# A single-core adaLN block with a top-2 expert layer: column halves asked for first in a tile, a shift leaves its bank at once, VectorE's work at the swiglu's begin spread out, slots' factors made ahead

## The chip, the cores and the metric

The kernel runs on one core of one Trainium2 chip. The metric is the device time of one launch in microseconds (us), the median of three runs. TensorE (PE) multiplies, VectorE (DVE) and ScalarE (ACT) work on rows of 128 partitions, GpSimd (POOL) and SyncE (SP) mostly issue DMAs.

## What is computed

The reference, cut to what matters (x has 4096 rows of D = 512, in two sequences; mod has six rows of 512 for each sequence):

```
sa, ca, ga, sb, cb, gb = rows of silu(c) @ wmod
ga, gb: |.| at least 0.25, sign kept
h = layernorm(x) * (1 + ca) + sa
# attention part, on h
qkv = rms(h) @ w_qkv.T ; q, k, v ; q, k = rms(q), rms(k)
w = exp(k)
y = sigmoid(q) * cumsum(w * v) / (cumsum(w) + 1e-6)
u, g = split(y @ w_swiglu.T)
x = x + ga * (h + u * silu(g) @ w_out.T)
# expert part
h = layernorm(x) * (1 + cb) + sb
gates = softmax of the 2 largest of 8 logits (h @ gate_w)
routed = sum over the 2 experts of gate * (gelu(h @ w1[e] + b1[e]) @ w2[e] + b2[e])
shared = gelu(h @ shared_w1 + shared_b1) @ shared_w2 + shared_b2
x = x + gb * (routed + shared)
```

All is fp32. Each product is made of three matmuls of rounded parts: both operands are split into a high part (ACT) and a low part (DVE), and PE multiplies hi*hi, lo*hi and hi*lo.

## The kernel before

Each engine has its own list of instructions, written out by hand in one order; engines wait for each other through semaphores. An instruction that waits holds back all that stands behind it on its engine. Memory is laid out by hand, too. The program has these stages, in order of time.

**Attention**, to about 365 us: 32 groups `g` of 128 rows. PE makes the products of a group, turns w and e by transposes (L761, `sums`), and ACT and DVE make norms, exponentials and cumulative sums. The six mod rows are made at the begin (`mod_row`, L716). For each sequence q a gain row and a shift row, spread over 128 partitions, stand in PSUM banks until DVE (`gain_a`, L1422) and ACT (`take_shift`, L1108 to L1110) copy them. The first call of `sums` on PE puts its transposes into those banks, so it waits for both copies of sequence 1. ACT calls `take_shift(1)` in its loop over groups at g == 1, behind `columns_hi(2)`.

**Swiglu**, to about 1456 us: passes "b" and "c" over the two halves of the swiglu's width, each with 8 tiles `t` of 512 rows and 8 blocks `s` of the width. For each block PE does 24 up products (L697 to L699), DVE multiplies the two halves (`s_t`, L1622), ACT rounds (`s_hi`), DVE makes `s_lo` (L1625), PE does 12 down products (L702 to L704) for the block before. In pass b, DVE has side work in fixed blocks of a tile: `rows_for_b(q)` at a sequence's first tile (the gain of the residual, `fix_gain` L1648 to L1651, then two products, L1659 and L1660), `token_stats` (L1631 to L1644) at s == 2, and `first_residual` at s == 3 to 6, whose last product is needed at the end of a tile. New weights come in pieces in the first tile (`w_blk`, L1418).

**Shared MLP**, about 1456 to 1676 us: 8 tiles of 512 rows, 4 blocks of the width each. The columns of the second norm's output are read back from HBM (`xs <- columns`, 1 MB) in halves of a tile, `load_half(h)` on SP (L518 to L527), h = 2t and 2t + 1, into three buffers. A load waits until PE has used up the half that the buffer held (`xs_free`), and in SP's list it stands behind other loads and stores: the rows `graw`, `h_rows`, the residual out and in (`second_norm_out`, `r_t`), `columns` (`hT_out`). The last tile's second norm (`LAST`) is finished here: PE turns rows to columns (`rows_to_hT`, L869), which waits for DVE's low part of the piece before (`hT_lo`, L1874), since both use one bank; in DVE's list `hT_lo(LAST, 2)` and `hT_lo(LAST, 3)` stand in tile 1 behind `block_s(1, 0)` and `block_s(1, 1)` (`s_lo`, L1922), and these behind `evacuate_s(0)` (L1684, L1688), which waits for the residual rows `r_t`. POOL meanwhile makes the lists of slots.

**Routed experts**, about 1676 us to the end: 71 slots of 128 rows for one expert. Each slot is gathered (POOL), turned on PE (L938), multiplied up (L951, L953), turned (L965), multiplied down (L979 to L981), and scattered with an add (POOL). On DVE `slot_o(j)` first makes the row `gb_row` (L2012: the gain row of the slot's sequences) in one buffer, waiting for the product before (`o_ok`), then waits for the down product, then multiplies into `o_t` (L2024).

Of the kernel before, what the change touches and what calls it, by code (L numbers as in the profile page):

```python
# [12 lines left out]
ALU = mybir.AluOpType  # L13
# [3 lines left out]
P = 128  # L17
# [18 lines left out]
def build(nc, x_tok, c, wmod, w_qkv, w_swi, w_sh, w_exp, b1s, b1r, b2p, b2s, gate_w, ident, tri, rank, tokid, ebase,  # L36
          thr, jota, steps, dues, jcol_in, list0, zrows, out):
    N, D = x_tok.shape
# [5 lines left out]
    NSUB = TT // P  # L44
# [41 lines left out]
    with ctx:  # L86
# [74 lines left out]
        NR = len(rows_t)  # L161
        o_t = [at(f"o_t{i}", k, [P, D]) for i, k in enumerate((180, 164, 166, 168, 170, 182, 128, 130, 132, 134))]
        NO = len(o_t)
        gb_row = at("gb_row", 174, [P, D])
        gT_hi = at("gT_hi", 184, [P, 2, H], F32R)
        gT_lo = at("gT_lo", 186, [P, 2, H], F32R)
        p_t = [at(f"p_t{i}", 188 + 2 * i, [P, D]) for i in range(2)]
        late_rows = [o_t[0], o_t[5], p_t[0], p_t[1]]
        u_t = at("u_t", 200, [P, 2, H])
        gl_t = at("gl_t", 202, [P, 2, H])  # L170
# [192 lines left out]
        def _(sp):  # L363
# [192 lines left out]
            sp.wait_ge(ffn["c"].ev_ok, NSUB * NT)  # L556
            sp.dma_start(b2_raw[:, :], b2p).then_inc(b_in, 16)
            gates_in(0)
            second_norm_out(LAST)
            for t in range(NT):  # L560
                if t == 1:
                    hT_out(LAST)
                if t == 4:
                    gates_out(LAST)
                    sp.dma_start(due_t[:, :, :], dues.rearrange("p (k j) -> p k j", k=3)).then_inc(tb_in, 16)
                if t == 3:
                    gates_out(LAST - 1)

                    sp.wait_ge(b2_ok, 1)
                    load_gain(1)  # L570
                if t + 1 < NT:
                    gates_in(t + 1)
                if t < LAST:
                    if t > 0:
                        load_half(2 * t + 2)
                    load_half(2 * t + 3)
                else:
                    half_left(2 * LAST - 2)
                    sp.dma_start(b1r_t[:, :], b1r).then_inc(b_in, 16)
                sp.wait_ge(ffn["s"].ev_ok, NSUB * (t + 1))  # L580
                sp.dma_start(tokens(out, t), r_t[:, :, :]).then_inc(out_st, 16)
                sp.wait_ge(out_st, 16 * (t + 1))
                if t < LAST:
                    load_r(x1_dram, t + 1)
# [468 lines left out]
        def _(act):  # L1053
# [143 lines left out]
            for g in range(NG):  # L1197
                square(g, 0)
                if g + 1 < NG:
                    columns_hi(g + 1)  # L1200
                if g == 0:
                    for n in range(1, NSUB):
                        square_h(n)
                    seed_root(0)
                if g == 1:
                    take_shift(1)
                if g in A_TURNS:
                    piece_hi(B0 + A_TURNS.index(g))

                t, n = g // NSUB + 1, g % NSUB  # L1210
                if g == 2:
                    square_h(NSUB)
                if 2 <= g < NG - NSUB + 1:
                    square_h(g + NSUB - 1)
                if g > 0 and n == 0:
                    seed_root(g // NSUB)
                    if t < NT:
                        seed_spread(t)
                square(g, 1)
                seed(g)  # L1220
                exponential(g, 0, w_t)
                exponential(g, 1, e_t)
                if g == 0:
                    seed_spread(1)
                if g >= 1:
                    reciprocal(g - 1)
                if g + 2 * NSUB < NG:
                    spread_of(g + 2 * NSUB)
                if 1 <= g < 5:
                    take_row(g + 1)  # L1230
                if g == NG - 2:
                    split(x_in, 16)
# [140 lines left out]
        def _(dve):  # L1373
# [279 lines left out]

            def rows_for_b(q):
                dve.wait_ge(bc_in, 16 * (4 if q == 0 else 6))
                if q == 0:
                    fix_gain(ga_t[0], tmp[0])
                    fix_gain(ga_t[1], tmp[1])
                then(nc.vector.tensor_tensor(a1_t[:, :], a1_t[:, :], ga_t[q][:, :], ALU.mult))  # L1659
                then(nc.vector.tensor_tensor(b1_t[:, :], b1_t[:, :], ga_t[q][:, :], ALU.mult))  # L1660

# [215 lines left out]
            for p in "bc":  # L1877
                for t in range(NT):
                    for s in range(NB):
                        if p == "c" and t >= 1 and s >= 5:  # L1880
                            hT_lo(t - 1, s - 5)
                        block_bc(p, t, s)
                        if p == "b":
                            if t == 0 and s == 0:
                                denominator(NG - 1)
                                sum_kv(NG - 1)
                            if t == 0 and s == 2:
                                quotient(NG - 1)
                                rows_for_b(0)
                            if t == T_SEQ and s == 2:  # L1890
                                rows_for_b(1)
                            if s == 2:
                                dve.wait_ge(r_in, 16 * (t + 1))
                                token_stats()
                            if 3 <= s < 3 + NSUB:
                                first_residual(t, s - 3)
                            if t == 0 and s == 7:
                                nc.vector.memset(prev[:, :, :], 0.0)
                                gate_weights()
                        else:  # L1900
                            hooks_c(t, s)
                        for i in pieces_at(p, t, s):
                            piece_lo(i)
                    if p == "c" and t >= 1:
                        hT_lo(t - 1, 3)
                    if (p, t) != ("c", LAST):
                        split(NC * (NT * PASS[p] + t + 1))
                    evacuate(p, t)
# [95 lines left out]
            def expert(j):  # L2004

                return dve.value_load(tab[0:1, 1, j:j + 1], min_val=0, max_val=(E - 1) * H)

            def slot_o(j):

                if j >= 1:  # L2010
                    dve.wait_ge(rt.o_ok, j)
                nc.vector.scalar_tensor_tensor(out=gb_row[:, :], in0=gbd_t[:, :], scalar=late_t[:, j:j + 1],  # L2012
                                               in1=gbs_t[0][:, :], op0=ALU.mult, op1=ALU.add).then_inc(rt.gr_ok, 1)
                dve.wait_ge(rt.gr_ok, j + 1)
                dve.wait_ge(rt.dn, j + 1)
                if j == 1:
# [5 lines left out]
                if j >= NO:  # L2022
                    dve.wait_ge(sc_st[(j - NO) % NA], 16 * ((j - NO) // NA + 2))
                nc.vector.scalar_tensor_tensor(out=o_t[j % NO][:, :], in0=bank_o[j % 2][:, :], scalar=gate_t[:, j:j + 1],  # L2024
                                               in1=gb_row[:, :], op0=ALU.mult, op1=ALU.mult).then_inc(rt.o_ok, 1)


            dve.wait_ge(b_in, 32)
# [14 lines left out]
            for j in range(NSLOT):  # L2043
# [8 lines left out]
                    slot_g(j + 1)  # L2052
                if j in R_TURNS:
                    piece_lo(R0 + 14 + R_TURNS.index(j))
            slot_o(NSLOT - 1)


# [70 lines left out]
```

## Time and profile before

| what | value |
|---|---|
| median of 3 runs | 1939.67 us (1938.92 to 1943.29) |
| profiled execution: device time | 1936.98 us |
| profiled execution: span of the core | 1935.2 us, mean granted TensorE clock 0.995 |
| PE busy | 1893.0 us (98%) |
| DVE busy | 1279.0 us (66%) |
| ACT busy | 650.1 us (34%) |
| POOL busy | 284.7 us (15%) |

The profile is one execution; its span is the time from its first to its last instruction, its device time has 1.8 us more around it. A row of a timeline reads: start, duration, engine, line, operation, what goes out and in, and in brackets the idle time of the engine just before and what ended it. A row of a table of windows reads: the window, its length, the busy time of PE, of its weight loads, of DVE, ACT and POOL (each with its count of instructions), PE's granted clock, the busy share of the 16 DMA engines, GB/s. The lines are those of the kernel before.

### The profile page before, as it was taken

Reading aid. Unit: us, or ns where it says so; the run is one execution under the profiler, and the core shown is the slowest. Engines: PE = TensorE matmul, PEld = TensorE weight load, DVE = VectorE, ACT = ScalarE, POOL = GpSimd, SP = SyncE. Lnnn points to the kernel's source line nnn. Section 1 sums busy time; section 2 is a strip of 40 time slices with the busy share of each in tenths; the row PEclk is TensorE's granted clock in tenths of the full one; section 3 lists DMA queues with packets and bytes.
Section 4 is the critical chain, followed back from the end, with each engine's and each line's share of the span. In section 5 each row is a group of like instructions: output and inputs, shape, how many; then the busy total and the mean of one; then the engine's idle time right before and its main releaser. Section 6 shows DMA issues by size and latency. Waiting matters only on the chain.

```text
span 1935.2 us, 26114 instructions
## 1 busy us (share of the span) xinstructions
PE 1893.0 (98%) x8882; PEld 1536.5 (79%) x8882; DVE 1279.0 (66%) x2639; ACT 650.1 (34%) x1309; POOL 284.7 (15%) x251
## 2 busy tenths in 40 slices
PE   7999999999999999999999999999998999999998
PEld 4688888878888888888888888888886777788886
DVE  6789999875545554556356456557556565599997
ACT  4677776621111111123112212222222332344443
POOL 0000000000000000000001011011020230388885
PEclk9999999999999999999999999999998999999999
DMA  5313112321110211025012422312344776588886
GB/s 189 135 49 104 54 50 66 131 78 64 66 56 10 77 66 44 22 90 182 23 65 82 116 68 82 138 68 82 116 133 183 249 227 216 180 156 154 153 153 97
DMA packets 88990, 206.74 MB, mean 107 GB/s; under 512 B 9781, under 2 KB 26454, under 8 KB 81772
## 3 DMA queue, kind: packets, MB, share of 16 engines
q1 hardware_dynamic: 65292, 144.55, 21.8%
q0 software_dynamic: 23568, 60.51, 14.7%
q8 instruction: 74, 1.21, 0.3%
q14 instruction: 56, 0.46, 0.1%
HBM read 126.95 MB, written 80.51 MB: 107 GB/s over the span
## 4 chain that ended last, share of the span: by engine, by line
PE 81%; POOL 8%; issue 4%; DVE 4%; DMA 3%; ACT 1%; POOLq 0%; SPq 0%; DVEq 0%; ACTq 0%
PE bank L697 13%; PE bank L699 13%; PE bank L698 13%; PE bank L702 12%; PE bank L704 11%; PE bank L703 11%; POOL out L661 5%; POOL rows_t L651 3%; DMA xs<-columns 2%; PE bank L716 1%; PE bank L731 1%; PE bank L761 1%; PE bank L772 1%; PE bank L765 1%; PE bank L869 1%
## 5 line engine op out<-in xcount | busy, mean ns | idle before, releaser
L697 PE MATMUL bank<-x_hi,w_blk 128*128 128x512 f32 x1024 | 403.2, 394 | 3.4 <-DVE s_t L1622 2.3
L699 PE MATMUL bank<-x_hi,w_blk 128*128 128x512 f32 x1024 | 399.5, 390 | 0.0
L698 PE MATMUL bank<-x_lo,w_blk 128*128 128x512 f32 x1024 | 399.2, 390 | 0.0
L1622 DVE TENSOR_TENSOR s_t<-act_t,bank 128x512 f32<-128x512 f32 x128 | 87.9, 687 | 272.7 <-PE bank L699 259.1
L1239 ACT ACTIVATE s_hi<-s_t 128x512 fp32r<-128x512 f32 x128 | 80.9, 632 | 436.2 <-DVE s_t L1622 417.3
L697 PEld LDWEIGHTS bank<-x_hi,w_blk 128*128 128x128 f32 x1024 | 192.7, 188 | 43.1 <-DVE w_blk L1418 2.7
L699 PEld LDWEIGHTS bank<-x_hi,w_blk 128*128 128x128 f32 x1024 | 192.6, 188 | 40.8
L698 PEld LDWEIGHTS bank<-x_lo,w_blk 128*128 128x128 f32 x1024 | 192.7, 188 | 38.9
L702 PE MATMUL bank<-w_blk,s_hi 128*128 128x512 f32 x512 | 199.9, 390 | 0.0
L704 PE MATMUL bank<-w_blk,s_lo 128*128 128x512 f32 x512 | 199.4, 390 | 0.0
L703 PE MATMUL bank<-w_blk,s_hi 128*128 128x512 f32 x512 | 199.3, 389 | 0.0
L1237 ACT ACTIVATE act_t<-bank 128x512 f32<-128x512 f32 x128 | 76.4, 596 | 353.4 <-PE bank L699 349.7
L702 PE MATMUL bank<-w_blk,xc_hi 128*128 128x512 f32 x384 | 156.6, 408 | 3.6 <-DVE xc_lo L1488 2.8
L704 PE MATMUL bank<-w_blk,xc_lo 128*128 128x512 f32 x384 | 150.6, 392 | 0.0
L703 PE MATMUL bank<-w_blk,xc_hi 128*128 128x512 f32 x384 | 149.8, 390 | 0.0
L1625 DVE TENSOR_TENSOR s_lo<-s_t,s_hi 128x512 fp32r<-128x512 f32 x128 | 88.7, 693 | 89.4 <-ACT s_hi L1239 86.6
L608 POOL DMA_DIRECT2D raw<-w_swi x16 | 8.7, 546 | 895.6 <-DVE w_blk L1418 810.9
L623 POOL DMA_INDIRECT slot_list<-pay,pos x64 | 65.0, 1016 | 463.4 <-DVE pos L1758 446.0
L661 POOL DMA_INDIRECT out<-o_t,ids_t x71 | 112.9, 1590 | 42.4 <-DVE o_t L2024 20.1
L702 PEld LDWEIGHTS bank<-w_blk,s_hi 128*128 128x128 f32 x512 | 96.1, 188 | 20.5
L704 PEld LDWEIGHTS bank<-w_blk,s_lo 128*128 128x128 f32 x512 | 96.1, 188 | 20.2
L703 PEld LDWEIGHTS bank<-w_blk,s_hi 128*128 128x128 f32 x512 | 96.1, 188 | 19.9
(272 smaller groups left out, 3445.1 us busy)
## 6 DMA issues: line engine op xcount, KB each, us to landing
x_t<-y_scratch SPq DMA_DIRECT2D x16, 1024.0 KB, 5.1
residual<-r_t SPq DMA_DIRECT2D x16, 1024.0 KB, 4.3
r_t<-residual SPq DMA_DIRECT2D x16, 1024.0 KB
columns<-hT SPq DMA_DIRECT2D x16, 1024.0 KB, 6.3
xs<-columns SPq DMA_DIRECT2D x16, 1024.0 KB, 8.7
raw<-w_swi POOLq DMA_DIRECT2D x16, 768.0 KB, 4.4
y_scratch<-y_t SPq DMA_DIRECT2D x32, 256.0 KB, 2.7
r_t<-x_tok SPq DMA_DIRECT2D x8, 1024.0 KB
```

What stands on the lines that cost most here:

```text
L623: pool.indirect_dma_start(list_dram, bass.IndirectOffsetOnAxis(ap=pos[:, 2 * s + k:2 * s + k + 1], axis=0), pay[:, s, k, :], None).then_in ...
L661: pool.indirect_dma_start(out, bass.IndirectOffsetOnAxis(ap=ids_t[:, j:j + 1], axis=0), o_t[j % NO][:, :], None, compute_op=ALU.add).then_ ...
L697: nc.tensor.matmul(dst, w[:, 0, col:col + P], rhs_hi, start=start, stop=False)
L698: nc.tensor.matmul(dst, w[:, 0, col:col + P], rhs_lo, start=False, stop=False)
L699: return nc.tensor.matmul(dst, w[:, 1, col:col + P], rhs_hi, start=False, stop=stop)
L702: nc.tensor.matmul(dst, lhs_hi, w[:, 0, col:col + D], start=start, stop=False)
L703: nc.tensor.matmul(dst, lhs_hi, w[:, 1, col:col + D], start=False, stop=False)
L704: return nc.tensor.matmul(dst, lhs_lo, w[:, 0, col:col + D], start=False, stop=stop)
L1237: nc.scalar.activation(act_t[:, s % 2, :], bank[4 + 2 * s % 3][:, :], ACT.Silu).then_inc(f.act_ok, 1)
L1239: nc.scalar.activation(s_hi[:, s % 3, :], s_t[:, s % 2, :], ACT.Copy).then_inc(f.sh_ok, 1)
L1622: nc.vector.tensor_tensor(s_t[:, s % 2, :], act_t[:, s % 2, :], bank[4 + (2 * s + 1) % 3][:, :], ALU.mult).then_inc(f.s_ok, 1)
L1625: nc.vector.tensor_tensor(s_lo[:, s % 3, :], s_t[:, s % 2, :], s_hi[:, s % 3, :].bitcast(F32), ALU.subtract).then_inc(f.sl_ok, 1)
```

## The change

Four edits, each of order, on three engines:

- SP asks for halves of columns first: `load_half(3)` ahead of the last tile's second norm out, and in tiles 1 to 6 `load_half(2t + 2)` at the top of the tile, ahead of `hT_out`, the gates and the next `graw`; `load_half(2t + 3)` keeps its place.
- ACT takes sequence 1's shift out of its bank at g == 0, behind the two exponentials.
- DVE in the first tile of pass b: `rows_for_b(0)` goes to s == 1 and fixes only its own sequence's gain (the other is fixed in `rows_for_b(1)`, tile 4), `token_stats` to s == 3 and `first_residual` to s == 4 to 7.
- DVE in the routed stage: the row `gb_row` is made by a function of its own, `slot_gain(j)`, at the end of the loop's turn before, into one of two buffers.

```diff
@@ buffers
-        gb_row = at("gb_row", 174, [P, D])
...
+        gb_row = p_t
@@ SP, shared MLP
             gates_in(0)
+            load_half(3)
             second_norm_out(LAST)
             for t in range(NT):
+                if 0 < t < LAST:
+                    load_half(2 * t + 2)
                 if t == 1:
                     hT_out(LAST)
...
                 if t + 1 < NT:
                     gates_in(t + 1)
-                if t < LAST:
-                    if t > 0:
-                        load_half(2 * t + 2)
+                if 0 < t < LAST:
                     load_half(2 * t + 3)
-                else:
+                if t == LAST:
                     half_left(2 * LAST - 2)
@@ ACT, attention
-                if g == 1:
-                    take_shift(1)
...
                 exponential(g, 0, w_t)
                 exponential(g, 1, e_t)
                 if g == 0:
+                    take_shift(1)
                     seed_spread(1)
@@ DVE, rows_for_b
                 dve.wait_ge(bc_in, 16 * (4 if q == 0 else 6))
-                if q == 0:
-                    fix_gain(ga_t[0], tmp[0])
-                    fix_gain(ga_t[1], tmp[1])
+                fix_gain(ga_t[q], tmp[0])
@@ DVE, pass b
+                            if t == 0 and s == 1:
+                                rows_for_b(0)
                             if t == 0 and s == 2:
                                 quotient(NG - 1)
-                                rows_for_b(0)
                             if t == T_SEQ and s == 2:
                                 rows_for_b(1)
-                            if s == 2:
+                            first = 3 if t == 0 else 2
+                            if s == first:
                                 dve.wait_ge(r_in, 16 * (t + 1))
                                 token_stats()
-                            if 3 <= s < 3 + NSUB:
-                                first_residual(t, s - 3)
+                            if first < s <= first + NSUB:
+                                first_residual(t, s - first - 1)
@@ DVE, routed experts
+            def slot_gain(j):
+                if j >= 2:
+                    dve.wait_ge(rt.o_ok, j - 1)
+                if j < 2:
+                    dve.wait_ge(ffn["s"].ev_ok, NSUB * LAST + 3 + j)
+                nc.vector.scalar_tensor_tensor(out=gb_row[j % 2][:, :], in0=gbd_t[:, :], scalar=late_t[:, j:j + 1],
+                                               in1=gbs_t[0][:, :], op0=ALU.mult, op1=ALU.add).then_inc(rt.gr_ok, 1)
             def slot_o(j):
-                if j >= 1:
-                    dve.wait_ge(rt.o_ok, j)
-                nc.vector.scalar_tensor_tensor(out=gb_row[:, :], in0=gbd_t[:, :], scalar=late_t[:, j:j + 1],
-                                               in1=gbs_t[0][:, :], op0=ALU.mult, op1=ALU.add).then_inc(rt.gr_ok, 1)
                 dve.wait_ge(rt.gr_ok, j + 1)
                 dve.wait_ge(rt.dn, j + 1)
...
                 if j in R_TURNS:
                     piece_lo(R0 + 14 + R_TURNS.index(j))
+                slot_gain(j)
             slot_o(NSLOT - 1)
```

PE's and POOL's lists are the same before and after. In the rows of order below the numbers of lines of the changed kernel are two or three higher for the same instruction.

On ACT in the attention's first groups, before (w_t and e_t are the exponentials of group 0, sv_a the statistics of the next tile of rows, xc_hi the columns of group 2):

```order
L1158 ACTIVATE e_t_52<-bank,rk_a 128x512 [waits rk_ok_first]
L1127 ACTIVATE sv_a<-va_a 128x4 [waits va_ok_first]
L1128 ACTIVATE sv_a<-sv_a 128x4 [waits act_chain]
L1169 ACTIVATE junk_170,sum_t<-xr 128x512 [waits mv_ok_first,h_ok_first,xa_in]
L1141 ACTIVATE junk_100,ms_a<-bank 128x512 [waits ms_ok_first,mm_first]
L1116 ACTIVATE xc_hi<-bank 128x512 [waits mm_first,tr_ok_first]
L1110 ACTIVATE shift_a_98<-bank 128x512 [waits mod_mm]
```

And in the changed kernel:

```order
L1161 ACTIVATE e_t_52<-bank,rk_a 128x512 [waits rk_ok_first]
L1113 ACTIVATE shift_a_98<-bank 128x512 [waits mod_mm]
L1130 ACTIVATE sv_a<-va_a 128x4 [waits va_ok_first]
L1131 ACTIVATE sv_a<-sv_a 128x4 [waits act_chain]
L1172 ACTIVATE junk_169,sum_t<-xr 128x512 [waits mv_ok_first,h_ok_first,xa_in]
L1144 ACTIVATE junk_100,ms_a<-bank 128x512 [waits ms_ok_first,mm_first]
L1119 ACTIVATE xc_hi<-bank 128x512 [waits mm_first,tr_ok_first]
```

The copy of the shift moves from behind xc_hi to right behind the second exponential; three small rows on sum_t and mv_a between the two are not shown.

On DVE in the first tile of pass b, blocks 1 and 2, before (the rows from L1554 are `quotient`, those from L1648 `rows_for_b(0)`; of each gain's four rows the first stands here):

```order
L1622 TENSOR_TENSOR s_t<-act_t,bank 128x512 [waits act_ok_b,up_b]
L1625 TENSOR_TENSOR s_lo<-s_t,s_hi 128x512 [waits sh_ok_b]
L1418 TENSOR_TENSOR w_blk<-raw_83,w_blk 128x1536 [waits w_hi_ok]
L1622 TENSOR_TENSOR s_t<-act_t,bank 128x512 [waits act_ok_b,up_b]
L1625 TENSOR_TENSOR s_lo<-s_t,s_hi 128x512 [waits sh_ok_b]
L1554 TENSOR_TENSOR den_t_59<-den_t_59,rec_t 128x512 [waits y_st,sum_ok_first,rec_ok_first]
L1648 TENSOR_SCALAR tmp_114<-ga_t_110 128x512 [waits bc_in]
L1648 TENSOR_SCALAR tmp_115<-ga_t_111 128x512 [waits dve_chain]
L1659 TENSOR_TENSOR a_t<-a_t,ga_t_110 128x512 [waits dve_chain]
L1660 TENSOR_TENSOR b_t<-b_t,ga_t_110 128x512 [waits dve_chain]
L1631 BN_STATS stat<-r_t 128x6 [waits r_in,dve_chain]
```

And in the changed kernel:

```order
L1624 TENSOR_TENSOR s_t<-act_t,bank 128x512 [waits act_ok_b,up_b]
L1627 TENSOR_TENSOR s_lo<-s_t,s_hi 128x512 [waits sh_ok_b]
L1650 TENSOR_SCALAR tmp_114<-ga_t_110 128x512 [waits bc_in]
L1659 TENSOR_TENSOR a_t<-a_t,ga_t_110 128x512 [waits dve_chain]
L1660 TENSOR_TENSOR b_t<-b_t,ga_t_110 128x512 [waits dve_chain]
L1420 TENSOR_TENSOR w_blk<-raw_83,w_blk 128x1536 [waits w_hi_ok,dve_chain]
L1624 TENSOR_TENSOR s_t<-act_t,bank 128x512 [waits act_ok_b,up_b]
L1627 TENSOR_TENSOR s_lo<-s_t,s_hi 128x512 [waits sh_ok_b]
L1556 TENSOR_TENSOR den_t_59<-den_t_59,rec_t 128x512 [waits y_st,sum_ok_first,rec_ok_first]
L1420 TENSOR_TENSOR w_blk<-raw_82,w_blk 128x1536 [waits w_hi_ok]
L1624 TENSOR_TENSOR s_t<-act_t,bank 128x512 [waits act_ok_b,up_b]
L1633 BN_STATS stat<-r_t 128x6 [waits r_in]
```

The rows for sequence 0 stand one block earlier, those for the other gain (ga_t_111) are gone from here, and the statistics start behind the next block's s_t instead of ahead of it.

On SP where the shared MLP begins, before (xs_89 is the buffer of half 3, graw the gates of a tile, h_rows and residual the last tile's second norm going out):

```order
L504 DMA graw<-gate_rows 40x512 [waits g_st]
L484 DMA h_rows<-hrow 128x512 [waits h_ok_norm_2] x4
L486 DMA residual<-r_t 128x4x512 [waits x1_ok_norm_2]
L439 DMA r_t<-residual 128x4x512 [waits x1_st]
L504 DMA graw<-gate_rows 40x512 [waits g_st,gin_ok]
L527 DMA xs_89<-columns 128x2048 [waits hT_st,xs_free]
L581 DMA out<-r_t 128x4x512 [waits ev_ok_s]
```

And in the changed kernel:

```order
L505 DMA graw<-gate_rows 40x512 [waits g_st]
L528 DMA xs_89<-columns 128x2048 [waits hT_st,xs_free]
L485 DMA h_rows<-hrow 128x512 [waits h_ok_norm_2] x4
L487 DMA residual<-r_t 128x4x512 [waits x1_ok_norm_2]
L440 DMA r_t<-residual 128x4x512 [waits x1_st]
L505 DMA graw<-gate_rows 40x512 [waits g_st,gin_ok]
L584 DMA out<-r_t 128x4x512 [waits ev_ok_s]
```

The load of half 3 moves ahead of the last norm's rows out and of the residual out and in.

## Rows read from the trace of the kernel before

**Rows 1.** The page: busy time of each engine.

```profile
PE 1893.0 (98%) x8882; PEld 1536.5 (79%) x8882; DVE 1279.0 (66%) x2639; ACT 650.1 (34%) x1309; POOL 284.7 (15%) x251
```

**Rows 2.** Timeline of the attention's begin: PE, ACT, DVE.

```profile
46.13 0.63 PE L761 MATMUL bank<-ident_t,w_t 128*128 128x128 f32 x4 [3.25 <-issue]
...
42.12 0.20 ACT L1127 ACTIVATE sv_a<-va_a 128x4 f32<-128x4 f32 x1 [1.73 <-DVE va_a L1439]
...
45.44 0.59 ACT L1110 ACTIVATE shift_a<-bank 128x512 f32<-128x512 f32 x1
...
53.96 0.59 ACT L1184 ACTIVATE wmod_t<-bank 2x512 f32<-2x512 f32 x1 [0.42 <-PE bank L716]
...
41.99 0.68 DVE L1422 TENSOR_SCALAR gain_a<-bank 128x512 f32<-128x512 f32 x1
```

**Rows 3.** The swiglu's first tile: timeline of PE and DVE, then windows.

```profile
405.25 0.47 PE L697 MATMUL bank<-x_hi,w_blk 128*128 128x512 f32 x1 [2.28 <-DVE s_t L1622]
...
385.65 1.76 DVE L1418 TENSOR_TENSOR w_blk<-raw,w_blk 128x1536 fp32r<-128x1536 f32 x1 [4.81 <-ACT w_blk L1106]
...
391.25 0.42 DVE L1648 TENSOR_SCALAR tmp<-ga_t 128x512 f32<-128x512 f32 x1
...
393.61 0.43 DVE L1648 TENSOR_SCALAR tmp<-ga_t 128x512 f32<-128x512 f32 x1
...
397.44 2.47 DVE L1631 BATCH_NORM_STATS2 stat<-r_t 128x6 f32<-128x512 f32 x4
...
404.43 0.68 DVE L1622 TENSOR_TENSOR s_t<-act_t,bank 128x512 f32<-128x512 f32 x1
...
404.00:408.00 4.00, 2.75 (x9) 2.22 (x10) 3.23 (x6) 2.49 (x3) 0.53 (x1) 0.78 0.46 134
408.00:412.00 4.00, 4.00 (x16) 3.20 (x15) 3.37 (x4) 0.57 (x2) 0.53 (x1) 0.79 0.15 63
```

**Rows 4.** Shared MLP, tile 1: timeline of PE, SP, DVE, then windows.

```profile
1493.56 0.80 PE L697 MATMUL bank<-xs,w_shr 128*128 128x512 f32 x1 [7.74 <-DMA xs<-columns]
...
1480.90 0.37 SPq L486 DMA_DIRECT2D residual<-r_t  x1
1485.22 0.37 SPq L439 DMA_DIRECT2D r_t<-residual  x1
...
1486.17 0.33 SPq L527 DMA_DIRECT2D xs<-columns  x1
...
1491.16 1.29 DVE L1684 TENSOR_TENSOR tmp<-bank,gbs_t 128x512 f32<-128x512 f32 x2 [3.13 <-DMA r_t<-residual]
...
1497.90 0.69 DVE L1922 TENSOR_TENSOR s_lo<-s_t,s_hi 128x512 fp32r<-128x512 f32 x1 [1.60 <-ACT s_hi L1253]
1498.51 0.68 DVE L1874 TENSOR_TENSOR hT<-bank,hT 128x512 fp32r<-128x512 f32 x1
...
1494.00:1498.00 4.00, 4.00 (x13) 3.12 (x13) 2.36 (x5) 1.45 (x3) 0.00 (x0) 0.50 0.19 71
1498.00:1502.00 4.00, 4.00 (x20) 3.28 (x19) 3.59 (x16) 1.57 (x3) 0.00 (x0) 0.94 0.56 205
```

**Rows 5.** Shared MLP, tiles 3 and 4: timeline of PE and SP, then windows.

```profile
1551.79 0.50 PE L697 MATMUL bank<-xs,w_shr 128*128 128x512 f32 x1 [1.56 <-DMA xs<-columns]
...
1578.45 0.50 PE L697 MATMUL bank<-xs,w_shr 128*128 128x512 f32 x1 [1.37 <-DMA xs<-columns]
...
1534.16 2.56 SPq L527 DMA_DIRECT2D xs<-columns  x2
...
1538.00:1542.00 4.00, 4.00 (x19) 3.31 (x18) 1.92 (x2) 2.84 (x5) 3.39 (x3) 1.00 1.11 370
```

**Rows 6.** Routed experts: timeline of DVE and PE, then a window.

```profile
1687.84 0.75 DVE L2012 SCALAR_TENSOR_TENSOR gb_row<-gbd_t,late_t,gbs_t 128x512 f32<-128x512 f32 x1 [0.99 <-issue]
...
1694.48 0.49 PE L951 MATMUL bank<-w_all,xT_hi 128*128 x1 [0.61 <-issue]
...
1740.00:1760.00 20.00, 20.00 (x118) 17.29 (x117) 18.79 (x35) 8.07 (x18) 16.34 (x13) 1.00 0.86 154
```

More of the change, by code:

```diff
@@ L2024, in slot_o @@
                 nc.vector.scalar_tensor_tensor(out=o_t[j % NO][:, :], in0=bank_o[j % 2][:, :], scalar=gate_t[:, j:j + 1],
-                                               in1=gb_row[:, :], op0=ALU.mult, op1=ALU.mult).then_inc(rt.o_ok, 1)
+                                               in1=gb_row[j % 2][:, :], op0=ALU.mult, op1=ALU.mult).then_inc(rt.o_ok, 1)
             dve.wait_ge(b_in, 32)
```

## The prediction

> **What bounds the kernel now.** I read the page first: TensorE is busy 98% of the span of 1935.2 us, DVE 66%, ACT 34% [rows 1]. Idle PE and a lowered PE clock together are therefore all that an edit of order can win: 42 us of idle time. So next I took PE's timeline and looked for the rows whose bracket shows an idle time, then for the windows whose granted clock is below 1. Four places answer to the four edits: 3.25 us at 46.13 [rows 2], 2.28 us at 405.25 with a half clock behind it [rows 3], 7.74 us at 1493.56, again with a half clock, and 1.56 and 1.37 us in tiles 3 and 4 [rows 4, 5], and idle pieces of about half a us where the slots begin [rows 6]. Behind each of the first two PE is full for long stretches, so what is won there is carried to the end.
>
> **The shift (ACT).** PE stops at 46.13 - 3.25 = 42.88. Its transposes wait for the gain row, ready at 41.99 + 0.68 = 42.67, and the shift, ready at 45.44 + 0.59 = 46.03 [rows 2]: only the shift is late. Moved behind the second exponential, it falls into ACT's idle time of 1.73 us ahead of 42.12, which is longer than its 0.59, so it costs ACT nothing and is done at about 41.0 [rows 2]. PE goes on at 42.9: 3.25 won. ACT's rows behind it move up only by about 0.48 (the shift was 0.59 with its overlap), since they follow from DVE's statistics. The row that ACT copies for the next mod product (53.96, after an idle time of 0.42) would be ready at 53.96 - 0.42 - 0.48 + 0.59 = 53.65, and PE, now 3.2 us early less its own slack, wants it about 0.3 sooner. I take 2.9; ends 2.4 (another such wait in the groups behind) and 3.3 (none).
>
> **VectorE at the swiglu's begin.** PE stops at 402.97 and waits for s_t of block 3, which starts at 404.43 since the ten rows of `rows_for_b(0)` (391.25 to 397.44) and the statistics (397.44 to about 402.7) stand ahead of it [rows 3]. In the change the first gain's four rows (393.61 - 391.25 = 2.36) and the two products (397.44 - 393.61 - 2.36 = 1.47) make 3.8 us, and they fall into the 4.81 us that DVE waits ahead of w_blk at 385.65 [rows 3], as their inputs are asked for long before. The statistics go behind s_t of block 3. So this s_t starts at 404.43 - 6.19 (rows) - 5.31 (statistics to w_blk: 404.43 - 397.44 less w_blk's 1.7) = 392.9 at the earliest, and PE wants it at 402.97. The statistics then end at about 400.4, ahead of s_t of block 4, which is wanted about 8 us after that of block 3. Won: the 2.28 of idle time, and the clock that falls behind it. The two windows behind it show 0.78 and 0.79: 4 x 0.22 + 4 x 0.21 = 1.72 us of full speed lost [rows 3]. Together 4.0; I take 4.1 with the small waits around it. What is late next: `first_residual`'s last part is now at s = 7, 2.7 us of DVE nearer to the tile's end; PE needs DVE there only some 8 us after its last up product, so I cost it at nothing (bound: 1.5 if that cover is gone). The other gain is fixed in tile 4, 2.36 us more of DVE, in a block in which DVE has more than 3 us idle: nothing. Range 2.5 to 4.2.
>
> **Column halves, tile 1 (SP).** The load of half 3 is issued at 1486.17 and PE waits for it from 1485.82 to 1493.56 [rows 4]. SP could have issued it some 15 us before; the change does so, and this wait goes. But PE has another one close by. In its list L869 for the last tile's last piece stands 7 us behind (1500.55), and waits for `hT_lo(LAST, 2)` on DVE, which ends at 1498.51 + 0.68 = 1499.19 [rows 4]. DVE's way to it starts when r_t has landed, at 1491.16, and holds 1499.19 - 1491.16 - 1.60 = 6.43 us of work (the 1.60 is a wait for ACT that goes) [rows 4]. r_t is issued at 1485.22 behind the residual's way out and that isn't changed. It no longer shares the DMA engines with the half, so it lands between 1485.22 + 4.32 = 1489.5 (as the residual's store of the same size: 1480.90 to 1485.22) and 1491.16; I take 1490.6. Then PE goes on at L869 at 1490.6 + 6.43 + 0.15 = 1497.2 instead of 1500.55: 3.35 won. It stops at 1485.82 + (1500.55 - 1493.56 - 2.4) = 1490.4, so it is idle for 6.8 us again, and its clock falls again. That cost 2.4 before: half of 1493.56 to 1498, and 4 x 0.06 [rows 4]; before it was paid ahead of 1500.55, now behind. 3.35 - 2.4 = 1.0 is what I take; ends 0.3 (r_t as before) and 3.4 (the clock holds). The edit looks as if it gave back 7.74 + 2.4 = 10.1.
>
> On this clock the windows show 0.50 behind the idle time of 7.74 us [rows 4] and 0.78 behind that of 2.28 [rows 3]. The Trainium skill, page "TensorE: Matmul & The Clock Gate", section "HAM oscillation — how this bites in real kernels", says that bursts of products behind a DMA wait start cold each time; by it a wait that is only moved pays for the clock again. The two falls here agree. By the rule tile 1 gives 1.0; if the clock held, 3.4.
>
> **Column halves, tiles 3 and 4.** Both waits (1.56 and 1.37) are for the second half of a tile, whose own release by PE isn't moved [rows 5]. Of the two issues at 1534.16 the first is the moved one: an earlier request takes its 1 MB out of the crowd, if the engines have room. From 1538 to 1542 they are at 1.11 with 370 GB/s [rows 5]: full, partly with GpSimd's lists of slots. In tile 3 the first half could go only 2 us sooner, in tile 4 some 4 us. I take 0.3 and 1.0, together 1.3; ends 0 (the queue's total is the same) and 2.9 (both go).
>
> The Trainium skill, page "Trainium Kernel Development and Optimization", section "Key Constraints", says that DMAs issued by SP, ACT and GpSimd run on the same 16 DMA engines and interleave. By it an earlier request doesn't add bandwidth, and the gain here would be near 0; the trace's share of 1.11 agrees.
>
> **Slots' factors.** Where the slots run, PE is busy 20.00 of 20 us and DVE 18.79 [rows 6]: PE bounds, and what DVE does in another order can win nothing but at the begin. There DVE is late: 0.99 us ahead of gb_row at 1687.84, and PE shows 0.61 at 1694.48 and two more such pieces [rows 6]. The factor made a turn ahead takes 0.75 off DVE's way from down product to free bank. Of about 1.5 us in those pieces I take 0.7; ends 0 and 1.5.
>
> **Sum.** 2.9 + 4.1 + 1.0 + 1.3 + 0.7 = 10.0. The profiled execution would go from 1936.98 to 1927.0. The median of the runs shown is 2.7 higher than that execution, so it goes from 1939.67 to 1929.7.
>
> **Rivals.** (a) All of the shared stage's stalls go: if r_t or DVE comes much sooner than I think, 2.9 + 4.1 + 10.1 + 2.9 + 0.7 = 20.7, median 1919. For it: the largest stall's releaser is xs alone. Against: the chain from r_t to L869, in which each piece has a row. (b) Gains are taken back by other waits: PE comes early to places that were covered, above all to the store and load chains of the shared stage, whose times are set by DMA. If the shared stage gives nothing and half of the first two are lost, 3.5 + 0.7 = 4 or less: median 1936 to 1939.7. Against: PE is full between the places, and DVE is 66% busy. (c) Slower: each slot's expert index is read by DVE right behind the new place of the factor and so directly ahead of the product into o_t. If the read's latency, so far covered by the wait for the down product, is exposed in each slot, DVE becomes the bound. It has 1.21 us free in 20, or 0.2 per slot, so this decides from 0.2 per slot. The idle time of 0.99 at 1687.84 is the nearest row for such a latency: (0.99 - 0.2) x 70 = 55, less the 9 of the other parts: median about 1985. Against: 0.99 stands once and the same reads in the window from 1740 leave DVE 94% busy, so they are mostly not exposed. (d) The edits do their work off PE's way everywhere except the first two: 7.0 alone, median 1932.7; this lies in my range.
>
> **How the numbers follow.** My forecast 0.80 (with (d) in it), (a) 0.08, (b) 0.08, (c) 0.04. The sum of lower ends is 2.4 + 2.5 + 0.3 + 0 + 0 = 5.2, median 1934.5; the sum of upper ends 3.3 + 4.2 + 3.4 + 2.9 + 1.5 = 15.3, median 1924.4. A part of (a) belongs into the range, as its price is known: 1922 to 1935. A difference of 0.2% (3.9 us) is about what runs of this kernel can tell. Faster than that: 0.80 + 0.08, and of (b) little: 0.88. Within: 0.08. Slower: 0.04, all of it (c).
>
> **What would show it.** The shift at about 40.4 to 41.0 and L761 at 42.9 with no bracket. Ahead of block 3's up products at 402 no idle time, and clock 1.00 in the windows behind. In tile 1 no wait for xs, but one of 6 to 7 us ahead of the second L869, named as DVE's hT, and a clock of 0.50 behind it; if that wait is missing, (a) holds. In tiles 3 and 4 waits for xs that are shorter but there. Slots at the same pace, 71 of them; if it is longer by 0.2 and more, (c). I am wrong too if `first_residual` in block 7 makes PE wait at the end of the first tile, or if r_t lands later than at 1491.

## The result, and the profile after

The changed kernel takes 1932.37 us in the median (1929.89 to 1934.7, 15 runs) against 1940.42 (1935.32 to 1943.29, 15 runs) for the kernel before: ratio 0.9959, 95% interval 0.9952 to 0.9966, so 6.6 to 9.3 us faster, 8.0 in the middle. Forecast were 10.0. The profiled execution took 1934.11, with a span of 1932.3; that is above its kernel's median, where the one of before was below it, so the two spans differ by 2.9 only. The traces show where this comes from.

The page's busy times are hardly others than in [rows 1]:

```profile
PE 1895.0 (98%) x8882; PEld 1538.4 (80%) x8882; DVE 1274.9 (66%) x2639; ACT 650.4 (34%) x1309; POOL 284.3 (15%) x251
```

Timeline of the attention's begin, ACT and PE, the places of [rows 2]:

```profile
42.20 0.60 ACT L1113 ACTIVATE shift_a<-bank 128x512 f32<-128x512 f32 x1
44.04 0.20 ACT L1130 ACTIVATE sv_a<-va_a 128x4 f32<-128x4 f32 x1 [1.24 <-DVE va_a L1441]
...
44.66 0.66 PE L764 MATMUL bank<-ident_t,w_t 128*128 128x128 f32 x4
```

The shift stands in ACT's idle time, and the transposes have no bracket. (All is 1.93 us later here than before: TensorE's clock was 0.96 in the first 40 us, where it was 1.00 in the profile before.)

The swiglu's begin, DVE's timeline and two windows, the places of [rows 3]:

```profile
382.74 0.69 DVE L1660 TENSOR_TENSOR b_t<-b_t,ga_t 128x512 f32<-128x512 f32 x1
384.61 1.76 DVE L1420 TENSOR_TENSOR w_blk<-raw,w_blk 128x1536 fp32r<-128x1536 f32 x1 [1.18 <-ACT w_blk L1109]
...
391.87 0.68 DVE L1624 TENSOR_TENSOR s_t<-act_t,bank 128x512 f32<-128x512 f32 x1
...
393.86 2.46 DVE L1633 BATCH_NORM_STATS2 stat<-r_t 128x6 f32<-128x512 f32 x4
...
400.00:404.00 4.00, 4.00 (x20) 3.30 (x19) 3.27 (x5) 0.63 (x1) 0.53 (x1) 1.00 0.39 121
404.00:408.00 4.00, 4.00 (x19) 3.34 (x18) 2.13 (x4) 0.60 (x1) 0.00 (x0) 1.00 0.19 75
```

The gain's rows lie in the former idle time (4.81 is now 1.18), s_t is at 391.87, and PE is full with its clock at 1.00.

Tile 1 of the shared MLP, PE, DVE and windows, the places of [rows 4]:

```profile
1492.12 1.09 PE L872 MATMUL bank<-ident_t,hrow 128*128 128x128 f32 x4 [7.03 <-DVE hT L1874]
...
1485.63 1.29 DVE L1684 TENSOR_TENSOR tmp<-bank,gbs_t 128x512 f32<-128x512 f32 x2 [2.89 <-DMA r_t<-residual]
...
1490.69 0.69 DVE L1925 TENSOR_TENSOR s_lo<-s_t,s_hi 128x512 fp32r<-128x512 f32 x1
1491.29 0.68 DVE L1874 TENSOR_TENSOR hT<-bank,hT 128x512 fp32r<-128x512 f32 x1
...
1492.00:1496.00 4.00, 3.88 (x12) 3.23 (x13) 3.45 (x19) 0.69 (x2) 0.00 (x0) 0.50 0.63 235
1496.00:1500.00 4.00, 4.00 (x18) 3.27 (x17) 2.73 (x5) 2.36 (x4) 0.53 (x1) 0.93 0.83 287
```

The wait for xs is gone, and 7.03 us for hT stand in its place, 7 us further on in PE's list, with the half clock behind them.

Tile 4, PE, SP and windows [rows 5], and the first gathered rows:

```profile
1572.59 0.80 PE L700 MATMUL bank<-xs,w_shr 128*128 128x512 f32 x1 [3.68 <-DMA xs<-columns]
...
1554.83 0.32 SPq L528 DMA_DIRECT2D xs<-columns  x1
...
1572.00:1576.00 4.00, 3.41 (x8) 2.74 (x9) 0.50 (x1) 0.45 (x1) 0.00 (x0) 0.50 0.90 332
1576.00:1580.00 4.00, 4.00 (x14) 3.12 (x14) 2.90 (x7) 1.73 (x4) 0.00 (x0) 0.69 0.28 109
...
1667.49 1.23 PE L941 MATMUL bank<-ident_t,rows_t 128*128 128x128 f32 x8 [1.00 <-DMA rows_t<-h_rows,ids_t]
```

Tile 3's wait of 1.56 is gone, tile 4's has grown from 1.37 to 3.68 and now costs clock as well. The first gather is waited for, as it wasn't before. The slots' pace is as it was: in the window from 1740 to 1760 PE is busy 20.00 of 20 us again, DVE 18.47.

A second reading is used below: the start of one and the same instruction in a kernel's trace less its start in the trace of before, in us. The instructions are kv_t of group 0 (42.59 before), s_lo of DVE at 380.15, 443.91, 1461.84, 1527.30 and 1665.63, and PE's last product (1925.70). The difference of two neighbours in a row of the table is what that stretch gave: the changed kernel goes from -1.12 to -5.27 between 380.15 and 443.91, so the swiglu's begin gave 4.15 us. Each row is one execution.

| kernel | 42.59 | 380.15 | 443.91 | 1461.84 | 1527.30 | 1665.63 | 1925.70 |
|---|---|---|---|---|---|---|---|
| changed | +1.93 | -1.12 | -5.27 | -5.27 | -6.31 | -3.16 | -3.08 |
| all_again | -0.31 | -3.31 | -7.45 | -7.44 | -8.54 | -7.33 | -7.30 |
| shift_alone | +2.57 | -0.48 | -0.51 | -0.50 | -0.81 | +1.58 | +1.01 |
| swiglu_alone | +0.05 | +0.09 | -4.06 | -4.05 | -3.66 | +0.42 | +0.29 |
| halves_alone | -0.36 | +1.29 | -0.31 | -0.32 | -1.54 | -0.52 | -0.52 |
| slots_alone | +2.83 | +4.44 | +2.84 | +2.85 | +2.64 | +1.85 | +0.91 |
| half3_only | -0.65 | -3.65 | -7.80 | -7.80 | -8.85 | -4.54 | -5.51 |

### The profile page after: what moved, and what is told of

The parts are those of the page before. It is cut to its first block, busy times and chain, and to the rows that moved or that the text cites. A ratio compares the mean times of both kernels' runs of the same rounds, so it can differ in the third digit from the quotient of the medians.

```text
span 1932.3 us, 26114 instructions
## 1 busy us (share of the span) xinstructions
PE 1895.0 (98%) x8882; PEld 1538.4 (80%) x8882; DVE 1274.9 (66%) x2639; ACT 650.4 (34%) x1309; POOL 284.3 (15%) x251
## 4 chain that ended last, share of the span: by engine, by line
PE 83%; POOL 7%; issue 4%; DVE 3%; DMA 2%; ACT 1%; POOLq 0%; SPq 0%; DVEq 0%; ACTq 0%
PE bank L700 13%; PE bank L702 13%; PE bank L701 13%; PE bank L705 12%; PE bank L707 11%; PE bank L706 11%; POOL out L664 4%; POOL rows_t L654 3%; PE bank L719 1%; DMA xs<-columns 1%; PE bank L734 1%; PE bank L764 1%; PE bank L768 1%; PE bank L775 1%; PE bank L872 1%
```

## The experiments

All ratios are to the kernel before, run on the same chip as the kernel in question; the chip isn't the same for all groups of runs.

**Each edit by itself**, in the kernel before; each kernel has one of the four edits of the list under "The change".

> Only the shift's copy on ScalarE moves. Theory 1 (the forecast's own terms add up, each at its place): TensorE's idle time of 3.25 us ahead of the first transposes is gone and the work that follows to the end of the attention stands about 3 us earlier, 2.9 faster in the median (ratio about 0.9985). Theory 2 (what is won early is partly given back where DMAs, not TensorE, set the pace, above all in the shared MLP's tiles 1, 3 and 4 and at the first gathers): less than 1.5 us in the median, with longer waits for xs in the shared MLP.

Measured: ratio 0.9976 (0.9966 to 0.9987), 4.6 us, so theory 2's "less than 1.5" is out. The stretch from 42.59 to 380.15 gave 3.05 in the trace; tiles 3 and 4 lost 2.4 in it.

> Only VectorE's side work at the swiglu's begin is spread out. Theory 1: the idle time of 2.28 us and the half clock behind it are gone, 4.1 us from there on, and 4.1 faster in the median (ratio about 0.998). Theory 2: the same 4.1 at the end of the swiglu, but under 2.5 at the end of the kernel, since the waits in the shared MLP grow.

Measured: 0.9984 (0.9972 to 0.9995), 3.1 us; 4.15 in its stretch, and 4.1 us lost in tiles 3 and 4, the picture of theory 2. The interval (1.0 to 5.4 us) has room for both theories.

> Only SyncE's loads of column halves move. Theory 1: tile 1 gives 1.0 us (the wait for xs becomes one of about 7 us for hT ahead of the last transposes, with the half clock behind it), tiles 3 and 4 give 1 to 1.5, 2.3 faster in the median. Theory 3 (the order of the loads itself makes tile 4 worse: the second half lands later because the first half, now asked for 2 to 3 us earlier, meets the slot lists' writes): in tile 4 a wait of 3 to 4 us with a lowered clock behind it, tile 3's wait gone, and in all no gain or up to 3 us slower. If tile 4's wait is 1 to 1.5 as in the kernel before, the long one was this one execution's chance or needs the other edits.

Measured: 0.9995 (0.9984 to 1.0005). Tile 1 gave 1.22; waits of 7.05 for hT and, in tile 4, 2.90 for xs with a clock of 0.57 behind it, none in tile 3. That is theory 3's picture; whether the moved loads are its cause is asked below.

> Only the slots' factors are made a turn ahead. Theory 1: up to 1 us at the first slots, the pace of 3.45 us per slot unchanged, 0.7 faster in the median, within what can be told from no change. Rival: the read of the expert's index ahead of the product into o_t is exposed, and the pace grows by 0.2 or more per slot, 10 us or more in all.

Measured: 0.9987 (0.9975 to 0.9998), 2.5 us; the slots gave 0.94 (1.85 to 0.91), and PE is busy 20.00 of 20 us from 1740 to 1760, so the read of the index isn't exposed. One profile each can't say where the rest of the 2.5 is from.

Two of these traces show something that I had not asked for. In halves_alone and slots_alone the stretch from 42.59 to 380.15 is 1.6 us longer than before, and the next one 1.6 shorter. Windows of halves_alone behind the shift's wait and behind the swiglu's, then one of the kernel before behind the shift's:

```profile
44.00:48.00 4.00, 2.23 (x14) 2.14 (x15) 1.77 (x8) 3.05 (x11) 0.00 (x0) 0.87 0.06 12
48.00:52.00 4.00, 4.00 (x13) 2.61 (x12) 3.86 (x7) 3.13 (x7) 0.00 (x0) 0.70 0.93 356
...
404.00:408.00 4.00, 1.72 (x9) 1.24 (x7) 3.27 (x5) 1.57 (x2) 0.53 (x1) 1.00 0.15 22
```

```profile
48.00:52.00 4.00, 4.00 (x15) 1.97 (x14) 3.83 (x9) 3.01 (x5) 0.00 (x0) 1.00 0.89 317
```

The same idle time of 3.25 us is followed by a lowered clock in two traces (halves_alone, slots_alone) and by none in two others (before, swiglu_alone). Of the four that still have the wait of 2.28 us the clock fell behind it in before and shift_alone and not in the other two. Each of the two waits costs its idle time always and 1.6 us of clock in two of its four executions here.

**The changed kernel once more.**

> The changed kernel as it is, once more, for a second profile beside the others of this chip. If the long wait in tile 4 (3.68 us) belongs to the new order, it is seen again at 3 to 4 us with the clock at half behind it; if it is chance (a kernel with the old order showed 3.71 too, others 0.48 to 2.10), it is anywhere from 0 to 4. The wait of 1.0 us for the first gathered rows: again if it belongs to the change, gone if chance. Tile 1's wait for hT of 7.0 us is there in any case. Median about 8 us below the kernel before.

Measured: 0.9947 (0.9934 to 0.996). Tile 1 waits 7.00 for hT, tile 4 3.12 for xs (clock 0.57 behind it), the first gather 0.94: all three are seen again. The last needs a limit. Seven other kernels with the moved loads (halves_alone and the six below that start from the changed kernel and keep them) show no wait for the first gather.

**The even halves back in their old place** (only half 3 early).

```diff
             for t in range(NT):
-                if 0 < t < LAST:
-                    load_half(2 * t + 2)
...
                 if 0 < t < LAST:
+                    load_half(2 * t + 2)
                     load_half(2 * t + 3)
```

> The changed kernel, but the loads of the even halves 4 to 14 stand where they stood before; only half 3 is asked for early. Theory M (moving the even halves only shifts the wait from tile 3 to tile 4): tile 3's wait of 1.6 us for xs is back, tile 4's is 0.5 to 2.1 us instead of 2.9 to 3.7, with little or no lowered clock behind it, and in sum tiles 3 and 4 cost the same within 1 us; ratio to the kernel before 0.995 to 0.996 as the changed kernel's. My forecast's theory (the moved loads give 1.3 us): 1.3 us more at the end of tile 4 than with them moved. If tile 4 shows 3 us here too, its wait has nothing to do with the moved loads.

Measured: 0.995 (0.9934 to 0.9965). PE's timeline:

```profile
1566.59 0.50 PE L697 MATMUL bank<-xs,w_shr 128*128 128x512 f32 x1 [1.59 <-DMA xs<-columns]
1572.36 0.75 PE L697 MATMUL bank<-xs,w_shr 128*128 128x512 f32 x1 [4.11 <-DMA xs<-columns]
```

Theory M falls: tile 3 has no wait here either, and tile 4 has two, together 5.7 us. swiglu_alone, with all loads in the old order, shows the same pair (1.94 and 3.71); before, shift_alone and slots_alone show 1.6 in tile 3 and 1.37, 2.10 and 0.48 in tile 4. So with the old order two patterns are seen, with the moved loads one (0 and 2.9 to 3.7). From 1527.30 to 1665.63 the old order lost 0, 2.4, 4.1, 4.3 and won 0.8; the moved one lost 3.2, 1.2 and 1.0. The means differ by 0.2 us, the runs by nothing that can be told. hT_early, both_early and columns_out_late below, all with the moved loads and other edits in tile 1 only, agree: no wait in tile 3, 3.2 to 4.5 us in tile 4, and 1.6, 2.9 and 1.6 us lost from the end of tile 2 on.

**Tile 1: VectorE's order.** First only hT_lo, then s_lo too (the line with block_s, which only both_early has), ahead of the wait for the residual rows:

```diff
             def evacuate_s(t):
...
+                if t == 0:
+                    block_s(1, 0)
+                    hT_lo(LAST, 2)
                 dve.wait_ge(f.dn, NB_S * (t + 1))
                 dve.wait_ge(r_in, 16 * (2 * NT + t + 1))
```

> The changed kernel with hT_lo(LAST, 2) put ahead of VectorE's wait for the residual rows. My theory (the stall of tile 1 is VectorE's order, not the load of the half): TensorE doesn't stop at the last transposes but goes on for the 12 products behind them, then waits some 3.3 us for s_lo and the first banks; 3.7 us less idle time, and 2.4 more if the clock holds through the shorter idle time. 3.7 to 6 us faster than the changed kernel (ratio to the kernel before 0.9925 to 0.994). Rival (the 7.0 us are a wait for r_t or DMA that any later instruction meets too): idle time stays at 6 to 7 us in tile 1, ratio as the changed kernel's 0.996.

Measured: 0.9952 (0.9939 to 0.9965). PE's timeline:

```profile
1489.27 0.50 PE L705 MATMUL bank<-w_shr,s_hi 128*128 128x512 f32 x1 [3.11 <-DVE s_lo L1925]
...
1513.66 0.50 PE L700 MATMUL bank<-xs,w_shr 128*128 128x512 f32 x1 [4.15 <-DMA xs<-columns]
```

The window behind the first of these waits has the full clock (1.00):

```profile
1488.00:1492.00 4.00, 2.73 (x12) 2.23 (x13) 3.59 (x17) 0.00 (x0) 0.00 (x0) 1.00 0.62 232
```

> As hT_early, and the low part of tile 1's block 0 (s_lo) ahead of the residual rows too. My theory: down(1, 0) can follow the evacuation bank by bank, idle time in tile 1 under 1 us, no half clock: 8 us less at the end of tile 1. Of it 0 to 4 are lost in tile 2, whose halves of columns are asked for behind the residual rows' way out and in. In the end 4 to 8 faster than the changed kernel (ratio to the kernel before 0.992 to 0.994). If the whole 8 us come back as a wait for xs in tile 2, the loads were the bound after all, one tile later.

Measured: 0.9965 (0.9954 to 0.9977). PE's timeline, then SP's:

```profile
1487.79 0.51 PE L705 MATMUL bank<-w_shr,s_hi 128*128 128x512 f32 x1 [0.36 <-DVE r_t L1688]
...
1515.05 0.80 PE L700 MATMUL bank<-xs,w_shr 128*128 128x512 f32 x1 [7.59 <-DMA xs<-columns]
```

```profile
1494.42 0.36 SPq L440 DMA_DIRECT2D r_t<-residual  x1
1494.88 0.45 SPq L528 DMA_DIRECT2D xs<-columns  x1
1495.38 1.29 SPq L510 DMA_DIRECT2D columns<-hT  x2
...
1497.18 0.32 SPq L528 DMA_DIRECT2D xs<-columns  x1
```

In tile 1 the idle time went as my theory has it (7.0 to 3.11, and to 0.36), so the order on VectorE is the cause there. At the end of the tile hT_early had won 6.5 us and both_early 7.2. But tile 2 took all of it back, with 4.15 and 7.59 us of wait for half 5: issued at 1496.22 and at 1497.18, it landed 17.4 and 17.9 us later, behind 4 MB issued in the 3 us ahead of it. So both forecasts of the ratio were missed (0.9925 to 0.994, and 0.992 to 0.994): neither kernel is faster than the changed one.

**Columns out behind half 5**, on top of both_early.

```diff
                 if t == 1:
-                    hT_out(LAST)
...
                     load_half(2 * t + 3)
+                if t == 1:
+                    hT_out(LAST)
```

> As both_early, and the last tile's columns (2 MB, wanted only some 100 us later) go out behind the load of half 5 instead of ahead of it. Theory B (tile 2's wait of 7.6 us is the queue of 5 MB that SyncE issues within 3 us, residual rows, half 4, columns out, half 5): without those 2 MB half 5 lands 6 to 8 us sooner, tile 2's wait is 0 to 2 us, and the 8 us won in tile 1 reach the end of tile 2; 6 to 9 us faster than the changed kernel, ratio to the kernel before about 0.992. Rival (half 5 is late for another reason, its own release or the residual rows): tile 2's wait stays above 5 us and the ratio at 0.9965.

Measured: 0.9925 (0.9911 to 0.9938), median 1923.77. SP's timeline, then the one wait over 1 us that PE has left in tiles 1 to 7:

```profile
1498.24 0.44 SPq L528 DMA_DIRECT2D xs<-columns  x1
1498.73 1.21 SPq L510 DMA_DIRECT2D columns<-hT  x2
```

```profile
1565.21 0.57 PE L700 MATMUL bank<-xs,w_shr 128*128 128x512 f32 x1 [3.21 <-DMA xs<-columns]
```

Theory B holds: tile 2 shows no wait, and the stretch from 1461.84 to 1527.30 gave 8.9 us where the changed kernel's gave 1.0. The store's place was changed on top of the other two edits only; what it gives without VectorE's new order wasn't tried.

**Tile 4: the slot lists.** In lists_later two waits of GpSimd, one ahead of each list:

```diff
+            pool.wait_ge(xs_in[half_at(7)[0]], 16 * (half_at(7)[1] + 1))
             to_lists(LAST - 1)
...
+            pool.wait_ge(xs_in[half_at(9)[0]], 16 * (half_at(9)[1] + 1))
             to_lists(LAST)
```

> The changed kernel, where GpSimd writes the last two tiles' slot lists (8 indirect writes each) only when the second half of columns of tile 3, and of tile 4, has landed. Theory W (the small writes crowd the DMA engines while these halves are under way): the two halves land 6 to 11 us after their issue instead of 15 to 18, no wait for xs in tiles 3 and 4, clock 1.00 there, 2 to 6 us less at the end of tile 4. Theory S (the four transfers of 1 MB per tile fill the engines by themselves): the second halves land 14 us or more after their issue, and waits of 1 to 4 us are seen again.

Measured: 1.0 (0.9991 to 1.0009): all 8 us of the change are lost, where 2 to 6 more had been expected. SP's timeline, then GpSimd's:

```profile
1557.59 0.54 SPq L528 DMA_DIRECT2D xs<-columns  x1
```

```profile
1568.17 1.00 POOL L626 DMA_INDIRECT slot_list<-pay,pos  x1 [19.72 <-DMA xs<-columns]
```

GpSimd went on at 1568.17, so half 9, issued at 1557.59, had landed within 10.6 us, against 17.8 in the changed kernel (1554.83 to 1572.59). That speaks for theory W, but not for the small writes alone, as the wait also held back the loads behind them in GpSimd's list (1 MB of weights, thr, jota, steps). And what stood behind the list on GpSimd was late, and with it VectorE and TensorE. DVE's timeline, then PE's:

```profile
1587.06 0.42 DVE L1804 TENSOR_TENSOR tab_c<-bank,thr_t 128x256 f32<-128x256 f32 x1 [13.87 <-DMA steps_t<-steps]
```

```profile
1592.53 0.80 PE L707 MATMUL bank<-w_shr,s_hi 128*128 128x512 f32 x1 [11.30 <-DVE s_lo L1927]
```

In last_list only the second list waits, and the loads of thr, jota, steps and two weights stand ahead of it:

> The changed kernel, where only the last tile's slot list waits until the second half of tile 4 has landed, and the small loads that VectorE wants stand ahead of it in GpSimd's list. Theory W (the small writes hold up that half): tile 4 shows no wait for xs or one under 1 us and no lowered clock, 3.5 to 5 us less at the end of tile 4 than the changed kernel's two profiles, without the 11 us stall that lists_later had; ratio to the kernel before 0.993 to 0.994. If tile 4's wait stays at 3 us, the writes aren't its cause; if a wait for VectorE of several us stands in tile 5 or 6 again, the list itself is needed sooner than I think.

Measured: 0.9948 (0.9935 to 0.9962). GpSimd's timeline, then PE's:

```profile
1567.80 1.00 POOL L626 DMA_INDIRECT slot_list<-pay,pos  x1 [7.96 <-DMA xs<-columns]
```

```profile
1594.22 0.50 PE L699 MATMUL bank<-xs,w_shr 128*128 128x512 f32 x1 [2.60 <-DMA xs<-columns]
1597.45 0.79 PE L699 MATMUL bank<-xs,w_shr 128*128 128x512 f32 x1 [1.15 <-DMA xs<-columns]
```

Half 9, issued at 1554.08, had landed by 1567.80, within 13.7 us; here only the list's writes had been held back, so by my estimate they account for some 4 us (17.8 and 17.2 with them, in the two profiles of the changed kernel). Tile 4 has no wait, and 3 to 4 us are won at its end against the changed kernel's two profiles, about as expected. But tile 5 has two waits with the clock at 0.50 behind them, and loses 6.7: the cost shows a tile later, and the ratio missed its forecast. Why these halves are late wasn't tried.

**Both together**, the edits of columns_out_late and of last_list.

> The edits of columns_out_late and last_list together. If the causes are separate, the gains add: 10 to 13 us faster than the changed kernel, median about 1919 to 1922, ratio to the kernel before 0.989 to 0.991. If tile 3 or the gathers of the first slots become the next waits, half of it: ratio 0.992 to 0.994.

Measured: 0.9921 (0.9907 to 0.9934), median 1923.33. PE's timeline:

```profile
1508.95 0.51 PE L699 MATMUL bank<-xs,w_shr 128*128 128x512 f32 x1 [0.49 <-DMA xs<-columns]
...
1585.72 0.50 PE L699 MATMUL bank<-xs,w_shr 128*128 128x512 f32 x1 [1.65 <-DMA xs<-columns]
1588.92 0.50 PE L699 MATMUL bank<-xs,w_shr 128*128 128x512 f32 x1 [1.55 <-DMA xs<-columns]
```

The gains don't add: it stands 0.0004 below columns_out_late, within the interval. Both are about 15 us faster than the kernel before. Against the changed kernel they are 4 to 7 us faster by the ratios (0.9959, and 0.9947 when it was run again), 7 to 9 by the medians, which are from different chips.

## Why the prediction was right, term by term

- **Shift, 2.9.** The idle time gave 3.00 to 3.05 in the four traces of the table that have the edit, nearer to the upper end. What I left out is clock: it fell behind this wait in two of four traces without the edit, so by my estimate (half of 1.6) the edit is worth 0.8 more in the mean. shift_alone's 4.6 us (interval 2.5 to 6.6) agrees, though it can't show it.
- **Swiglu's begin, 4.1.** 4.15, 4.14 and 4.15 in three traces, with the clock in it. Where the clock holds behind the old wait it would be 2.5, an estimate from the 1.6 us that halves_alone and slots_alone show. `first_residual` in block 7 and the other gain in tile 4 cost nothing, as costed: the table doesn't move between 443.91 and 1461.84.
- **Tile 1, 1.0.** 1.04 and 1.10; the wait of 7.0 us for hT had been worked out as 6.8, and the clock fell again. (The prediction also took the fall behind 2.28 us for one that comes each time; it came in two of four traces, see the last section.) The step that carried it, that the last transposes are the next thing late, was shown by taking their wait away. Rival (a) is out. Even with VectorE in order the 8 us were not to be had before the columns' store was moved too, traffic that I hadn't counted.
- **Tiles 3 and 4, 1.3.** This is the term that was mis-sized. "An earlier request takes its 1 MB out of the crowd" bought nothing that can be seen: the two traces of the changed kernel lost 3.2 and 1.2 us there against before. The waits weren't "shorter but there" either: tile 3's went, tile 4's grew. And the moved load of tile 4 was issued only 2.1 us sooner in the tile (1551.89 after, 1562.17 before, with 8.17 us won up to there), not "some 4". That the engines are full with GpSimd's lists was right, and last_list shows that these writes hold up tile 4's second half (17.8 us from issue to landing with them, 13.7 without). The end at 0 was the better choice. Which of the two patterns an execution of the old order falls into stays open.
- **Slots, 0.7.** 0.94 to 1.25 in the eight traces that have the edit and no wait for the first gather. The two traces of the changed kernel itself wait 1.00 and 0.94 for it and lost 0.08 and 0.03, so there this term gave nothing. (shift_alone, without the edit, won 0.57 in this stretch, so a few tenths can be chance.) This is rival (b) on a small scale. The moved loads don't bring this wait by themselves, as seven kernels have them without it, and PE isn't early: its products release the gather, and in every trace it wants the rows 4.5 us after GpSimd issued it. In these two they landed after 5.7 and 5.6 us (1661.80 to 1667.49 in the first). Why stays open. Rival (c) is out: the pace didn't change.

With 3.05, 4.15, 1.05, 0 and 0, the sum is 8.2; 0.8 more for the shift's clock and 0.8 less for the swiglu's, each paid in half of the traces, leave it there. Measured were 8.0. The first three terms had been forecast at 8.0 and make up what was measured; the other two, 2.0 together, gave nothing in the changed kernel.

## What to carry to other kernels

When a wait's releaser is moved, look for the next instruction in the waiting engine's list that has a releaser of its own, and work out when that one comes: in tile 1 the named wait was 7.7 us and its removal gave 1.0. It took three edits (the load and a store nobody was waiting for on SyncE, and the order on VectorE) before the trace showed the 8 us in tiles 1 and 2, and each of the first two, as it was added, gave little but the next wait. A store that isn't wanted soon belongs behind the loads that are.

## What I had not expected of the hardware

The granted clock after a short idle time differs from execution to execution: behind the same 3.25 us it stayed at 1.00 twice and fell to 0.70 to 0.87 in windows of 4 us twice, and behind the same 2.28 us it fell twice and held twice. In each of the three traces that have both waits just one of them was paid for, 1.6 us each time. In the shared MLP it held at 1.00 behind an idle time of 3.11 us in tile 1 of hT_early, and fell to 0.65 behind 2.10 us in tile 4 of shift_alone. Behind the idle times of 7 us and more there it was 0.50 in every trace. A single profile can therefore misprice a short wait by the whole of its clock term.
